# Masks of the scores written into PSUM by ScalarE, and the layer norm's statistics a step later

## The reference, cut to what matters

```python
def local_attention(q, k, v):          # windows of 32 tokens, each sees itself and the one before
    ...
    mask = (it < jb) | (it > jb + w) | (jb == -1)
    sim = jnp.einsum('bhwie,bhwje->bhwij', bq, bk2) * QK_SCALE
    sim = jnp.where(mask, -jnp.finfo(sim.dtype).max, sim)
    attn = jax.nn.softmax(sim, -1)
    out = jnp.einsum('bhwij,bhwje->bhwie', attn, bv2)
...
for i in range(DEPTH):
    x = attn_layer(shift_tokens(x), Wqkv[i], q_scale[i], k_scale[i], Wo[i]) + x
    x = ffn_layer(shift_tokens(x), ln_g[i], ln_b[i], W1[i], b1[i], W2[i], b2[i]) + x
```

## Time and profile before

| | us |
|---|---|
| median of 3 runs | 3629.76 (3622.65 to 3633.49) |
| profiled execution, its own time | 3632.55 |
| its span | 3630.7 |
| first attention, up to the first projection of the layers | 445 |
| PE busy | 3457.8 |
| ACT busy | 3054.1 |
| DVE busy | 3008.1 |
| POOL busy | 2492.5 |

### The profile page before, as it was taken

One profiled execution on the slowest core, in us unless ns is written; L12 is line 12 of the kernel. 1 busy time (PEld: TensorE's weight loads), 2 busy tenths in 40 slices (PEclk: granted clock), 3 DMA queues, 4 the chain that ended last, 5 costly groups with the idle time before them and its releaser, 6 DMA issues. The chain is left out here.

```text
span 3630.7 us, 177745 instructions
## 1 busy us (share of the span) xinstructions
PE 3457.8 (95%) x70388; PEld 2913.2 (80%) x70388; DVE 3008.1 (83%) x7016; ACT 3054.1 (84%) x10549; POOL 2492.5 (69%) x2057
## 2 busy tenths in 40 slices
PE   8999999999999999999999999999999999999998
PEld 5666677888888888888888888888888888888777
DVE  8999988888888787887888878878888888888886
ACT  8999878888888888888888888888888888888775
POOL 0111287777778777787777877777777777787774
PEclk9999999999999999999999999999999999999999
DMA  2000011111111111111111111111111111111111
GB/s 101 7 13 11 13 51 53 46 39 45 51 53 48 41 43 48 51 55 42 43 41 52 55 45 45 41 41 52 53 46 47 39 45 50 45 42 47 45 45 42
DMA packets 177474, 160.59 MB, mean 44 GB/s; under 512 B 113933, under 2 KB 124813, under 8 KB 176397
## 3 DMA queue, kind: packets, MB, share of 16 engines
q1 hardware_dynamic: 176653, 149.22, 14.5%
HBM read 25.71 MB, written 4.19 MB: 8 GB/s over the span
## 5 line engine op out<-in xcount | busy, mean ns | idle before, releaser
L1544 POOL TENSOR_TENSOR a_rn<-a_ssqc,a_minus_half 128x16 f32<-128x16 f32 x384 | 1113.3, 2899 | 273.8 <-DVE a_ssqc L1751 268.9
L1428 ACT ACTIVATE late<-bank,a_negmax 128x64 f32<-128x64 f32 x3072 | 964.3, 343 | 138.6 <-DVE a_negmax L1705 137.5
L1562 POOL TENSOR_TENSOR a_r<-a_u,a_rn 128x512 f32<-128x512 f32 x768 | 800.6, 1043 | 181.7 <-DVE a_u L1733 136.0
L1428 ACT ACTIVATION_READ_ACCUMULATOR late<-bank,a_negmax 128x1 f32 x3072 | 728.8, 237 | 0.0
L1551 POOL TENSOR_TENSOR a_PN<-late,a_erec 128x256 f32<-128x256 f32 x768 | 487.7, 635 | 264.4 <-DVE a_erec L1758 252.9
L1717 DVE TENSOR_TENSOR a_u<-bank,a_rot_c 128x512 f32<-128x512 f32 x768 | 526.0, 685 | 155.7 <-ACT a_sq L1404 155.2
L1054 PE MATMUL bank<-ident,a_r 128*128 128x128 f32 x3072 | 467.1, 275 | 63.0 <-POOL a_r L1562 58.9
L1726 DVE TENSOR_TENSOR a_v<-bank,a_rot_s 128x512 f32<-128x512 f32 x768 | 524.3, 683 | 0.0
L1733 DVE TENSOR_TENSOR a_u<-a_u,a_v 128x1024 f32<-128x1024 f32 x384 | 470.5, 1225 | 25.9 <-DVE a_v L1726 0.5
L1404 ACT ACTIVATE a_sq<-bank 128x512 f32<-128x512 f32 x768 | 469.9, 655 | 19.8 <-PE bank L1013 19.3
L1411 ACT ACTIVATE a_QK<-bank 128x512 f32<-128x512 f32 x768 | 465.6, 607 | 4.3 <-PE bank L1054 2.1
(11 more groups left out here) (190 smaller groups left out, 7828.5 us busy)
## 6 DMA issues: line engine op xcount, KB each, us to landing
a_V_sh<-a_V_nat SPq DMA_DIRECT2D x384, 192.0 KB, 2.4
a_V_sh<-a_V_nat SPq DMA_DIRECT2D x192, 64.0 KB, 2.4
late<-in_qkv SPq DMA_DIRECT2D x20, 384.0 KB, 3.9
a_x_sh<-X SPq DMA_DIRECT2D x48, 128.0 KB
a_V_sh<-a_V_nat SPq DMA_DIRECT2D x192, 32.0 KB, 2.1
a_x_sh<-X SPq DMA_DIRECT2D x48, 127.0 KB
late<-X SPq DMA_DIRECT2D x47, 128.0 KB
late<-X SPq DMA_DIRECT2D x47, 127.0 KB
```

Source lines behind the costliest of these rows:

```text
L1428: ins = act.activation(E[:, s.par, k, :], scores[:, hp, col:col + KW], ACT.Exp, bias=negmax[:, s.par, k:k + 1], accum_out=esum[:, s.par, k ...
L1544: pool.tensor_tensor(rn[:, a.par, :], ssqc[:, a.par, :], minus_half[:, :], ALU.pow).then_inc(S["rn"], 1)
L1562: pool.tensor_tensor(heads(r[:, a.par, half]), heads(u[:, a.par, half]), rn[:, a.par, mm * 2 * HG:(mm + 1) * 2 * HG].unsqueeze(2).to_broad ...
```

## The change

Three things change in `all_layers`.

1. Masks. A second table, `plain`, holds the masks by score row; DVE casts it to bf16 once. At the end of ACT's exponentials of a pair a new step function `mask` waits until these exponentials are complete (`exp1`) and copies the table's rows for the next pair into both banks of `p_s`, 128 partitions by 512 columns. PE waits for this (`masked`) in place of `exp1` and starts with the score products, still start=False. The first pair and the last four, whose scores are formed outside the steps, keep PE's mask products: 379 pairs change.
2. Statistics move from step 0 to step 1, POOL's deviation from step 0 to step 1, the normalisation from step 1 to step 2, where PE's `turn` already is.
3. PE forms the second projection ahead of `turn` in step 2 and ahead of the `up` product in step 6.

```diff
+                    if filled:
+                        pe.wait_ge(S["masked"], s.k)
+                    else:
+                        for c in range(4):
+                            for e in range(2):
...
-                if p == P_VALUES:
-                    up(n, p, 0, 1, p_ta)
-                if p == P_TURN:
-                    turn(n)
-                project(n, p, 1)
+                project(n, p, 1)
+                if p == P_TURN:
+                    turn(n)
+                if p == P_VALUES:
+                    up(n, p, 0, 1, p_ta)
...
-                if s:
-                    ge(pe, S["exp1"], s.k)
-                logits(s, p_s)
+                logits(s, p_s, s is not None and s.k > 0)
...
+            def mask(s):
+                if s and s.k + 1 <= NI * NP - LAG_L - 1:
+                    act.wait_ge(S["exp1"], s.k + 1)
+                    if s.k == 0:
+                        act.wait_ge(S["plain"], 1)
+                    act.activation(p_s, A["plain"][:, 1 - s.half, :].unsqueeze(1).to_broadcast([P, 2, 4 * KW]), ACT.Copy).then_inc(S["masked"], 1)
...
                 exps(s, 1, 1, p_s)
+                mask(s)
...
-                if p == 0 and n >= 2:
+                if p == P_NORM and n >= 2:
                     deviation(n - 2)
...
-                if p == P_NORM:
-                    norm(n)
                 if p == P_X:
                     residual(n)
-                if p == 0:
+                if p == P_NORM:
                     stats(n)
+                if p == P_TURN:
+                    norm(n)
```

More of the change, by code:

```diff
@@ L130, in first_attention @@
         xn = sb("xn", [P, T])
-        masks_f = sb("masks_f", [P, 2, 4 * KW])
+        masks_f, plain_f = sb("masks_f", [P, 2, 4 * KW]), sb("plain_f", [P, 2, 4 * KW])
         raw = sb("raw", [P, G, 3 * CQ])
@@ L187, in _ @@
                         (w.out[:, :, :], dram["wo"][0]), (A["tabs_c"][:, :, :, :], dram["rot_cos"]),
-                        (A["tabs_s"][:, :, :, :], dram["rot_sin"]), (masks_f[:, :, :], dram["windows"])):
+                        (A["tabs_s"][:, :, :, :], dram["rot_sin"]), (masks_f[:, :, :], dram["windows"]), (plain_f[:, :, :], dram["plain"])):
                     sp.dma_start(dst, src).then_inc(S["weights"], 16)
@@ L363, in step @@
                         if half == 0:
-                            act.wait_ge(S["weights"], 144)
+                            act.wait_ge(S["weights"], 160)
                         ins = high_weights(act, A, raw[:, b - 3, :], b - 3, half)
@@ L511, in step @@
                         dve.tensor_copy(A["masks"][:, :, :], masks_f[:, :, :])
+                        dve.tensor_copy(A["plain"][:, :, :], plain_f[:, :, :]).then_inc(S["plain"], 1)
                         dve.tensor_copy(A["ident_b"][:, :], ident[:, :])
@@ L648, in layer_constants @@
     sb("masks", [P, 2, 4 * KW], BF16)
+    sb("plain", [P, 2, 4 * KW], BF16)
     sb("ident_b", [P, P], BF16)
@@ L1104, in outputs, with logits @@
                     ins.then_inc(S["o"], 1)
-            def logits(s, scores):
+            def logits(s, scores, filled=False):
                 if s:
@@ L1112, in logits @@
                     sides = (slice(0, 64), slice(64, P))
[L1113 to L1117, removed]
+                    if filled:
[3 more added lines that the diff above has]
+                            for e in range(2):
+                                rows = slice(WIN * c, WIN * c + WIN)
+                                pe.matmul(scores[rows, e, :], ident_b[sides[e], 64 * e:64 * e + WIN],
+                                          masks[sides[e], int(s.half > 0 or c > 0), :], start=True, stop=True, skip_group_check=True)
                     for hp in range(2):
@@ L1972, in _ @@
             end()
-LAYER_SEMS = ("xt xh xl x_loaded f_loaded qk_out0 qk_out1 pt pt_out v_out o_out o y pn0 pn1 exp0 exp1 logits r0 r1 "
+LAYER_SEMS = ("plain masked xt xh xl x_loaded f_loaded qk_out0 qk_out1 pt pt_out v_out o_out o y pn0 pn1 exp0 exp1 logits r0 r1 "
               "qkt0 qkt1 sq0 sq1 qk v max red u u_rot rec0 rec1 rn v_rot0 v_rot1 summed x_out weights w_hi w_lo raw0 raw1 scales "
@@ L2012, in tables @@
     windows = np.stack([np.concatenate([seen & (k >= WIN), seen] * 2, 1), np.concatenate([seen] * 4, 1)], 1)
+    first = np.arange(P)[:, None] < WIN
+    seen = (np.arange(P)[:, None] % WIN <= k) & (k <= np.arange(P)[:, None] % WIN + WIN)
+    plain = np.stack([np.concatenate([seen & (~first | (k >= WIN)), seen] * 2, 1), np.concatenate([seen] * 4, 1)], 1)
     half = np.arange(0, DH, 2, dtype=f)
@@ L2029, in tables @@
     return {"ident": eye, "causal": both_sides(causal).astype(f), "pick": both_sides(pick).astype(f),
-            "windows": np.where(windows, 0, NEG).astype(f), "rot_cos": both(np.cos(freqs)).astype(f),
+            "windows": np.where(windows, 0, NEG).astype(f), "plain": np.where(plain, 0, NEG).astype(f), "rot_cos": both(np.cos(freqs)).astype(f),
             "rot_sin": both(np.sin(freqs) * sign).astype(f)}
```

## The result

| | before | after |
|---|---|---|
| median, us | 3626.2 (beside after) | 3539.39 (3535.4 to 3542.2) |
| ratio, 95% interval | | 0.9759 (0.9736 to 0.9781) |
| profiled execution, us | 3632.55 | 3535.4 |
| its span, mean granted clock | 3630.7, 0.984 | 3533.6, 0.996 |
| ordinary iteration, us | 64.1 | 62.45 |

The account below looks back on a forecast made before the run. PE was taken to set the pace. Steps of 52.00 + 7.79 + 2.25 made 62.0 us an iteration against 64.1; 97 us over 46 iterations plus 5 at layer changes took 3632.55 to 3530, 8-in-10 range 3470 to 3600.

Parts of the forecast that it names:

- the 2.27 us of PE's waits: PE's waits in steps 0 and 1, 1.43 + 0.84 us an iteration, were to go with the later statistics.
- Masks off PE: Removing the eight mask products from PE saves 0.12 us a step, 0.96 an iteration, all on the path.
- loop B: PE to ACT to PE: score products, probability copy, mask copy, PE again; 6.67 us against PE's need of 6.50.
- Loop C: DVE to ACT to DVE: maxima, exponentials, mask, squares, cosines, next maxima; 6.77 us, setting the plain step.
- It fills 0.70 of the 0.71, so that wait goes: PE in step 6: the second projection, ahead of the feed-forward product that waited for ACT, removes the 0.71 us wait.
- Steps 6 and 7: Step 6 takes 8.18 us, mask ending at 8.05, PE ready at 7.90; step 7 takes 7.76, DVE's maxima late.
- Step 0: PE's transposes wait 0.92 us for the low part of x, the mask adds 0.11: 6.50 + 1.03 = 7.53.
- Layer changes: Iterations where weights change: 5 us gain counted, from DVE's longer DMA wait; rival that they lose more, 3590 to 3620, chance 0.13.
- Full gain: Rival: the loops through ACT and DVE don't close, 60.0 us an iteration, about 3445 us; chance 0.12.
- A dearer copy: Rival: ACT's mask copy into PSUM takes over 0.94 us and the change loses; 3730 us at 1.2; chance 0.08.
- Statistics that still wait: Rival: the DMA lands later than 14 us after the residual, leaving only the mask's part, 3668 us; chance 0.04.
- ScalarE as the bound: Rival: ACT has no slack, so each of 379 copies adds 0.74 us, giving 3808 us; chance 0.03.

Follow-up runs that it names:

- the copy in three steps: The whole change, but ACT copies the mask only for steps 3 to 5 and PE writes it in the others: 3485.18 us, and 3486.82 when repeated.
- the second copy: The whole change plus an equal ACT copy behind the mask copy, into an SBUF tile nobody reads: 3683.34 us, ratio 1.0139.
- the product first: The whole change with DVE's second product of step 6 moved ahead of that step's cosines and sines: 3512.84 us, ratio 0.9673.
- 3486 alone: The whole change without its mask part: PE writes all masks, statistics and PE's order as changed: 3486.05 us, and 3486.14 when repeated.
- 3660 alone: The kernel before with only the mask part added; statistics, deviation, normalisation and PE's order as before: 3660.22 us, ratio 1.008.

## Why the prediction was right, and where it was off

**Statistics.** Right. No wait stands ahead of L532, and the 2.27 us of PE's waits are gone: without copies step 1 is 6.62 in place of 9.02. The 14 us from the residual to the statistics are 14.5.

**Masks off PE.** Right: PE's need falls by about 0.1 us a step, as steps 3 to 5 of the copy in three steps show (0.12, 0.09, 0.10). One reading was wrong. The eight products are not 15 ns apart: in the trace they start 3 to 4 ns apart, within 24 ns, and 0.12 is the distance from the first of them to the first score product. That distance is the right price.

**The copy and its loops.** Right in mechanism, and nearly in size. The copy is 602 ns; loop B is 6.68 (6.67). Loop C, which the prediction had as the longer one at 6.77, is 6.68 too: its squares to cosines take 0.61, not 0.69. ACT's wait on itself, put at 0.05 without a row, is 0.03. That ACT's time had become dear is shown by the second copy, 3.2 of 4 us.

That the copy costs more than the eight products did is shown by the pair with and without it: 3539 against 3486. The steps say where. With the copy step 7 is 0.65 longer (8.52 against 7.87), step 2 0.29, step 0 0.12 and step 1 0.05; steps 3 to 6 are 0.03 to 0.11 shorter. So in a plain step loop and mask products nearly cancel, and the largest part of the price is one wait, DVE's `product` in step 6, that the prediction doesn't name: taking it away (3513) gives half of the 53 us back.

**PE's order.** "It fills 0.70 of the 0.71, so that wait goes" is the step that failed. In step 6 the order brings 0.25 us (8.82 to 8.57). The `up` product no longer waits, but the values behind it now wait 0.20 for ACT's copy of the outputs (L1025 above), with the masks' copies and without them (9.4 us in 46 iterations in both). The part on step 2 held, and is the larger half: 0.53.

**Steps 6 and 7.** Forecast 8.18 and 7.76, measured 8.51 and 8.52. The mask of step 6 ended 8.00 after the score products (8.05 was forecast), but PE was not ready at 7.90, as the forecast had it: it stood 0.5 behind the mask's end, since the values wait for ACT's copy of the outputs, with eight products behind the one that waits. That is 0.20 and 0.15 for the late start; 0.26 of the 0.61 has no mark in the timeline. The second is the wait for DVE's product, which the walk through the steps left out: it followed the late squares to DVE's maxima in step 7, and not to the product that stands between them: 0.70 and 0.16, 0.86 us in 46 iterations.

**Step 0.** Forecast 1.03 us of wait, measured 0.46: 0.30 at the transposes, which start 1.57 after the score products (1124.33 against 1122.76) in place of 1.27, and 0.16 for the mask. The 0.30 is what is left of the wait for the low part of x, which ends at 1124.18 (1123.49 + 0.69). It was real, but PE had lost 0.86 just before, and ACT and DVE had caught up. With the product first step 0 is 7.24. Waits that follow each other on the same path cover each other, so the errors belong together: steps 6 and 7 took 1.09 us more than forecast, step 0 took 0.57 less, the others 0.1 less, and 0.4 an iteration is what they cost.

**The sum.** The walk through the steps leaves out the 0.3 us of short waits that the prediction had counted in the iteration before, and gives no reason. Its own terms, 64.08 less 2.98, less 0.96, plus 2.25, make 62.4, not 62.0. That 62.4 is close to the 62.45 measured is luck, since the errors of steps 6, 7 and 0 lie elsewhere.

**Layer changes.** Counted at 5 us, they gave about 22: the 46 iterations took 97.7 us less (3009.4 to 2911.6), and 46 ordinary ones explain 75.9. The prediction's reason for its 5 us was wrong: DVE waited for the DMA no longer there: 2.9 us is the longest of all 46 waits, and in the iteration read above it was 2.33. Twenty iterations gain 2.3 to 4.6 us each in place of 1.65, those in which before's clock fell or DVE had tables to form behind its wait. The fallen clock alone made 1.0 to 1.2 us of each in the ones read (step 2 above, and an iteration of 65.1 with ordinary waits), some 20 us by that estimate. The 21 us that the runs of the kernel before give for the same difference of clock agree, but no run takes the clock apart from the wait that goes with it, so this share is an estimate. The forecast of 3530 came as close as it did by luck: 17 us too little here and 21 too much in the iterations (2.1 us in place of 1.65, 46 times) nearly cancel.

**The rivals.** Full gain (3445): refuted, though the version without copies comes halfway. A dearer copy: refuted by 602 ns. Statistics that still wait: refuted. ScalarE as the bound (3808): refuted as it stood, since the 379 copies cost 53 us, 0.14 each and not 0.74; with one more copy a step it nearly holds (0.4 of 0.5), and in steps 4 and 6 of the changed kernel ACT has no idle time left. The range is said to reach halfway to the full gain; 3470 lies 60 of the 85 us from 3530 to 3445. What was not asked is whether this part of the change should be there at all: the fastest kernels of the study have none of it, or have it in three steps.

## What to carry over

An instruction moved from the first engine to the second costs nothing only until it closes a loop through both: follow the late value to every reader in program order on each engine, also to those that stand between two that you know. Measure the parts of a change apart, since here one part (3486 alone) paid for another (3660 alone). And where a wait goes, look whether the clock of PE fell behind it: that gain is not in any wait's row.

## What the runs showed of the chip that was not expected

- PE's granted clock fell to half in an idle time of PE of 2.18 us, behind one of 0.98 in the same step, and stayed there from 957 to beyond 963; the same kernel's iterations with idle times of 1.27 and 0.68 mostly kept it.
- Over 23 runs of one unchanged kernel the time went with the mean granted clock: 3618.89 us at 0.992, 3637.13 at 0.983.
- The eight bf16 mask products (64*32, 64x256) start 3 to 4 ns apart, and the score product behind them starts 0.12 us after the first.
- ACT's copy of 128x512 from bf16 lasts 602 ns into PSUM and 615 ns into SBUF. The Trainium skill (ScalarE: Activation LUTs, "Step-by-step: what each stage is for") says that ScalarE writes PSUM with less latency than SBUF; the rows agree in sign, and the difference is 13 ns.
- PE starts 0.15 us after the end of the ACT instruction it waits for, of which the prediction had estimated 0.13.
